# First layer: all picked-expert tiles in one line of pairs behind the last scan; decay and r read from two PSUM banks, rows shifted by one

## What is computed

```python
# attention of layer 0 (RWKV form), per token, 16 heads of 16 x 16:
kv = kt[..., :, None] * vt[..., None, :]
o = einsum('bhk,bhkv->bhv', rt, S + u[None, :, :, None] * kv)
S = dt[..., None] * S + kv
# then group norm, gate, x = x + o @ Wo, h2 = rms_norm(x), x = x + gelu(h2 @ w1) @ w2
# feed-forward of layer 0: 2 shared experts, 4 of 16 routed experts per token
probs = softmax(xt @ router_w.T); topk_p, topk_i = top_k(probs, 4)
routed = einsum('tre,rhe->th', gelu(up_r) * gate[:, :, None], routed_down)
```

## Time and profile before

| | us |
|---|---|
| median of 3 runs | 5062.5 (5051.38 to 5066.56) |
| profiled execution | 5088.27 |
| its span | 5086.5 |
| mean granted PE clock of the span | 0.899 |
| first layer's scans | 52.3 to 2249 |
| second layer's first scan | 2683.7 |
| second layer's scans end | about 4384 |

### The profile page before, as it was taken

One profiled execution on the slowest core, in us unless ns is written; L12 is line 12 of the kernel. 1 busy time (PEld: TensorE's weight loads), 2 busy tenths in 40 slices (PEclk: granted clock), 3 DMA queues, 4 the chain that ended last, 5 costly groups with the idle time before them and its releaser, 6 DMA issues. The chain is left out here.

```text
span 5086.5 us, 64064 instructions
## 1 busy us (share of the span) xinstructions
PE 4041.3 (79%) x19024; PEld 2762.4 (54%) x19024; DVE 3733.9 (73%) x6383; ACT 2719.0 (53%) x5646; POOL 3369.3 (66%) x2370
## 2 busy tenths in 40 slices
PE   5777787887778887878448989888888888489994
PEld 1344554565445654556345555555555555368883
DVE  6888698678886888741008998988889888645677
ACT  1333643454345543546237777777777777245552
POOL 3456576576566766672358888888888888645552
PEclk7888887999889988989679999999999999699997
DMA  4233445444544446641662122221112211396788
GB/s 180 85 102 127 145 134 134 143 146 132 134 146 144 156 129 151 167 154 53 144 152 84 59 68 83 84 72 70 65 67 82 85 67 66 136 237 206 243 279 279
DMA packets 378773, 659.74 MB, mean 130 GB/s; under 512 B 43616, under 2 KB 235488, under 8 KB 368096
## 3 DMA queue, kind: packets, MB, share of 16 engines
q1 hardware_dynamic: 288576, 464.59, 28.7%
q0 software_dynamic: 89856, 191.05, 13.4%
HBM read 455.29 MB, written 250.25 MB: 139 GB/s over the span
## 5 line engine op out<-in xcount | busy, mean ns | idle before, releaser
L1687 POOL TENSOR_TENSOR c_dbx<-c_dtx,c_Brep 128x1024 f32<-128x1024 f32 x512 | 1202.5, 2364 | 183.2 <-DVE c_hs L1705 99.0
L1705 DVE TENSOR_TENSOR_SCAN c_hs<-psum,c_carry,c_dbx 128x512 f32<-128x512 f32 x768 | 937.3, 1266 | 120.0 <-ACT psum L1694 70.7
L1116 POOL TENSOR_TENSOR a_kv<-a_rk,a_kv 128x512 f32<-128x512 f32 x512 | 708.1, 1391 | 431.2 <-DMA a_kv<-v_rows 419.7
L1125 DVE TENSOR_TENSOR_SCAN a_S<-a_decay,a_carry,a_kv 128x513 f32<-128x513 f32 x512 | 804.2, 1571 | 153.3 <-POOL a_kv L1116 147.8
L1694 ACT ACTIVATE psum<-c_dt,c_cols 128x512 f32<-128x512 f32 x1024 | 697.2, 688 | 364.9 <-DVE c_hs L1705 359.2
L1721 PEld LDWEIGHTS psum<-ident,c_hs 128*128 128x128 f32 x4096 | 488.1, 144 | 392.2 <-DVE c_hs L1705 213.8
L1721 PE MATMUL psum<-ident,c_hs 128*128 128x128 f32 x4096 | 611.0, 283 | 108.9 <-DVE c_hs L1705 104.1
L962 POOL DMA_INDIRECT picked_results<-a_t_y,a_to_slot x336 | 386.8, 1151 | 421.4 <-ACT a_t_y L953 165.8
L1131 DVE TENSOR_TENSOR a_prod<-a_rk,a_S 128x512 f32<-128x512 f32 x512 | 454.9, 888 | 78.3 <-PE psum L1147 78.3
L2110 POOL DMA_INDIRECT results<-d_ys,d_to_row x320 | 312.0, 975 | 250.4 <-issue 140.0
L872 POOL DMA_INDIRECT picked_rows<-a_row,a_to_row x256 | 351.8, 1374 | 122.7 <-issue 42.5
(11 more groups left out here) (316 smaller groups left out, 8161.6 us busy)
## 6 DMA issues: line engine op xcount, KB each, us to landing
a_kv<-v_rows SPq DMA_DIRECT2D x512, 256.0 KB
c_Brep<-b_rows SPq DMA_DIRECT2D x64, 1024.0 KB, 4.8
a_t_rows<-picked_rows SPq DMA_DIRECT2D x336, 144.0 KB
d_xs<-sorted_rows SPq DMA_DIRECT2D x320, 128.5 KB
x<-picked_results POOLq DMA_DIRECT2D x64, 512.0 KB, 7.6
d_w<-results SPq DMA_DIRECT2D x64, 512.0 KB, 11.4
d_w<-in_d_experts SPq DMA_DIRECT2D x32, 768.0 KB
picked_rows<-in_picked_pad SPq DMA_DIRECT2D x80, 144.0 KB
```

The costliest lines, as they stand in the source:

```text
L1116: m_kv[g] = pool.mark(nc.gpsimd.tensor_tensor(kv[:, g % NV, 1:C + 1], rk[slot][:, 1, hb, :], kv[:, g % NV, 1:C + 1], ALU.mult))
L1125: m_scan[q] = dve.mark(nc.vector.tensor_tensor_scan(S[:, q % NS, :], decay[cq % 2][:, hb, :], kv[:, q % NV, :], carry[:, sq_:sq_ + 1], ALU ...
L1687: m_dbx[g] = m_dbx[g + 1] = pool.mark(nc.gpsimd.tensor_tensor(dbx[:, r:r + 2, :], dtx[slot][:, e, :].unsqueeze(1).broadcast_to([P, 2, C]), ...
L1705: m_scan[q] = dve.mark(nc.vector.tensor_tensor_scan(hs[:, q % NR, :], psum[:, DA + q % ND, :], dbx[:, q % NX, :], first, ALU.mult, ALU.add))
```

## The change

In the scan loop:

- kv, S and the product are shifted by one token: column 0 of k, v and decay is the last column of the chunk before (three small ACT copies a chunk, one in `rv`, one in `decay`, one in `ks`), a state has 512 columns, and no column 0 is kept apart.
- For each block of 16 steps ACT copies decay and r (128x512) into PSUM banks 6 and 5. The first 3 steps of a block (`COPIED`) read SBUF as before, the other 13 the banks.
- Keeping the carry goes from DVE to ACT.
- kv, S and prod have 8 buffers each, the fetch runs 5 steps ahead, `PACE` is 3200.
- The pool `G` has 3 banks (1, 2, 7) instead of 5.

Tiles:

- `SEGMENTS` = 8, 8: 144 tiles a segment, 288 in all, in 144 pairs. `tiles` is gone from the background. `pairs_of_tiles` runs behind the last scan, a straight line with one pair per iteration, stages shifted against each other, one bank for each of its four products. The copies of the rows and of the hidden transposes go from ACT to DVE. Twice an iteration it advances the background once: the last chunk's block, the combines of chunks 0 to 7, and the second layer's opening, which begins when chunk 0 is combined.
- The combines of chunks 8 to 15 go into the second layer's scan loop. That layer waits for every tile's result to be stored (`wait_left`), and for the sums of a chunk only when it loads that chunk.

The diff, cut:

```diff
-        NV, NS, NP = 6, 4, 6
-        kv, S, prod = brief("kv", [P, NV, C + 1]), brief("S", [P, NS, C + 1]), brief("prod", [P, NP, C])
+        NV, NS, NP = 8, 8, 8
+        kv, S, prod = brief("kv", [P, NV, C]), brief("S", [P, NS, C]), brief("prod", [P, NP, C])
...
-        OB, FD, G = 0, Banks(psum, 2, 1), Banks(psum, 3, 5)
+        FD, G, OB, RB, DB = Banks(psum, 0), Banks(psum, 1, 2, 7), 3, 5, 6
...
+            if c >= 1:
+                act.after(*scanned, *m_done["ready", c - 1])
+                act.mark(nc.scalar.copy(decay[slot][:, :, 0], decay[1 - slot][:, :, C]))
+                m_edge = act.mark(nc.scalar.activation(ks[slot][:, :, 0], ks[1 - slot][:, :, C], ACT.Copy, scale=chunk_mask[:, c:c + 1]))
...
+            m_v = act.mark(nc.scalar.copy(rv[1 - slot][:, :, 0], vT[:, :, C]))
...
+            def rows_turned(p):
+                i, bank = TB.take(pe)
+                pe.engine.wait_ge(s_tx[p % NTX], 32 * (p // NTX + 1))
+                for k in range(2):
+                    for kb in range(KB):
...
+                dve.after(m_y.get(p - NTX))
+                m_of[p] = dve.mark(nc.vector.tensor_copy(t_of[:, p % NTX, :, :], t_rows[:, p % NTX, :, D:]))
+                dve.after(m_T[p], m_up.get(p - 2))
+                m_xT[p] = TB.freed[i] = dve.mark(nc.vector.tensor_copy(t_xT[:, p % 2, :, :].rearrange("p k d -> p (k d)"), bank))
...
+            AHEAD = NTX - 1
+            for p in range(AHEAD):
+                fetch(p)
+            for s in range(total + 2):
+                if s < total:
+                    rows_turned(s)
                 if s >= 2:
...
+                    hidden_turned(s - 2)
+                pause()
+                if 1 <= s <= total:
+                    up(s - 1)
+                if s >= 2:
+                    down(s - 2)
+                    if s - 1 in begins:
+                        m_done["tiles", segment[s - 2]] = s - 1
+                if s + AHEAD < total:
+                    fetch(s + AHEAD)
+                pause()
...
-        CHAIN_RATE, BEFORE_RATE, NORM_RATE, SORT_RATE, LEAD = 3, 1.3, 1.5, 1.0, 3
-        PACE = 4400
+        CHAIN_RATE, BEFORE_RATE, NORM_RATE, SORT_RATE, LEAD = 3, 1.3, 1.5, 1.0, 5
+        PACE, COPIED = 3200, 3
...
-                    m_kv[g] = pool.mark(nc.gpsimd.tensor_tensor(kv[:, g % NV, 1:C + 1], rk[slot][:, 1, hb, :], kv[:, g % NV, 1:C + 1], ALU.mult))
+                    m_kv[g] = pool.mark(nc.gpsimd.tensor_tensor(kv[:, g % NV, :], ks[slot][:, hb, 0:C], kv[:, g % NV, :], ALU.mult))
...
+                    if v < COPIED:
+                        decays = decay[cq % 2][:, hb, 0:C]
+                    else:
+                        decays = psum[:, DB, :]
+                        dve.after(m_bank["decay"])
...
+                    m_scan[q] = dve.mark(nc.vector.tensor_tensor_scan(S[:, q % NS, :], decays, kv[:, q % NV, :], carry[:, sq_:sq_ + 1], ALU.mult, ALU.add))
...
-                    m_prod[q] = dve.mark(nc.vector.tensor_tensor(prod[:, q % NP, :], rk[cq % 2][:, 0, sq_ // DK, :], S[:, q % NS, 0:C], ALU.mult))
+                    m_prod[q] = dve.mark(nc.vector.tensor_tensor(prod[:, q % NP, :], r_t, S[:, q % NS, :], ALU.mult))
...
-                    dve.after(m_scan[q])
-                    m_kept[q] = dve.mark(nc.vector.tensor_copy(carry[:, q % steps - 3:q % steps + 1], S[:, q % NS - 3:q % NS + 1, C]))
+                    act.after(m_scan[q], m_start[0])
+                    m_kept[q] = act.mark(nc.scalar.copy(carry[:, q % steps - 3:q % steps + 1], S[:, q % NS - 3:q % NS + 1, C - 1]))
+                for name, lag, bank, source, m_read in (("decay", 3, DB, decay, m_scan), ("r", 4, RB, rs, m_prod)):
...
+                        m_bank[name] = act.mark(nc.scalar.copy(psum[:, bank, :], source[cq % 2][:, hb, 0:C]))
...
+        tail_done = [("plan", len(Z.SEGMENTS) - 1), ("scattered", last), ("out", last), ("final", 0)]
...
+            left.advance_all()
+            if is_done(*tail_done) and not is_done("second"):
...
-            wait_stored(sp.engine, 2)
             load_xa(0)
...
-            background = Background((AFTER_RATE, []), (MAIN_RATE, []), (SORT_RATE, []), (1.0, []), (1.0, []))
+            background = Background((AFTER_RATE, []), (MAIN_RATE, []), (SORT_RATE, []), (1.0, []), (1.0, []), (1.0, sums))
...
-            wait_stored(lane.engine)
+            wait_left(lane.engine)
...
-    SEGMENTS = [2, 3, 4, 4, 3]
+    SEGMENTS = [8, 8]
```

359 lines of the change are left out of this document (150 added, 209 removed).

## The result

The changed kernel takes **5007.8 us** (median of 4 runs, 5005.5 to 5009.0) against 5063.2 of the kernel before in the same comparison, a ratio of 0.989 [0.988, 0.991]. It is faster, but by 55 us (1.1%) where the forecast said 240, and lies above the forecast's range.

What follows compares the result with a forecast made beforehand. DVE was taken to bound the scan loop's quiet windows, PE some other stretches, no engine the whole. Scan loop -405, stretch between the scans +155, second layer +10 make -240 us: 4824 us, range 4671 to 4970.

Steps and rivals of the forecast that it cites:

- Tiles leave the loop, -0.25 us a step: Scan loop: without tiles and combines the step falls from 4.29 to 4.04 us, read from four tile-free windows.
- Banks, -0.20 and -0.21 us a step: Scan loop: 13 of 16 scans and products reading PSUM save 0.20 and 0.21 us a step.
- Carry to ACT, -0.09: Scan loop: moving the carry's copy off DVE saves 0.09 us a step; ACT has room for it.
- Wider rings: Scan loop: eight buffers give back some of the 0.15 us a step that products waited for PE's sums.
- The pool of three, between 0 and all: Scan loop: three background banks instead of five cost between nothing and all that the other edits save.
- 2.95 us of work: Scan loop: DVE's work falls to 2.95 us a step; with 0.55 of idle kept, the step is 3.5 us.
- the first rival: Scan loop: DVE alone sets the step at 3.2 us, giving 4671 us; chance 0.18.
- The budget: Scan loop: with 3200 columns a step, PE needs 3.6 us in packed stretches, so 3.5 is just possible.
- First half of the pairs, 266 us: Between the scans: 72 pairs at 3.0 us plus 50 us for the last chunk's block; range 228 to 290.
- Second half, 290 us: Between the scans: 72 pairs, 32 sums and the second layer's opening, bound by DMA; range 263 to 381.
- Second layer, +10 us: Second layer's scan loop: 32 sums moved in cost 10 us, bounds 0 and 41.
- idle banks: Scan loop: rival that held-up scans and products stay at 1.52 and 0.93 us, giving 5028 us; chance 0.05.

Runs made afterwards that it cites:

- e9: Kernel before with only the tiles and combines out of the scan loop, rows shifted by one token, and the changed kernel's work behind the last scan: 5195 us.
- e3: Changed kernel without the copies to the banks, so all scans and products read SBUF; pool of 3 kept: 5104 us.
- e6: Changed kernel with rings back at 6, 4 and 6 buffers and fetches 3 steps ahead: 5011 us.
- e2: Changed kernel with the old budget, PACE 4400 columns a step instead of 3200: 5180 us.
- e1: Changed kernel with the carry's copy back on DVE: 4974 us.
- e15: e11 with two more rests lengthened (five in all), banks serving 14 of 16 steps, and the carry's copy on ACT: 4867 us.
- e7: e1 with three background rests lengthened (centring matmul, gate's product, head norm's last product): 4968 us.
- e11: e7 with rings of 6, 4 and 6 buffers and fetches 3 steps ahead: 4946 us.
- e16: Changed kernel with five background rests lengthened and nothing else: 4897 us.
- e5: e3 with the two freed banks given to the background's pool, five instead of three: 5087 us.
- e18: Kernel before the change with the same five rests lengthened: 5073 us, ratio 1.002.

## Why the prediction was wrong, point by point

- *Tiles leave the loop, -0.25 us a step.* Too much: -0.15 (e9), 53 us of the loop. Half of the error is in how the windows were averaged: the first, 400 of 1050 us, lies at the start of the loop, where steps are short, and by its share of the loop they give 4.09 and not 4.04. The other half stays open.
- *Banks, -0.20 and -0.21 us a step.* The prices of the instructions were right (1274 and 665 ns), and so was their sum, 0.42. The rule of the Trainium skill weighed there (Perfetto Trace Analysis, Optimizing Scalar/DVE Operations), about 60 ns for a DVE access on SBUF and 125 on PSUM, so 65 ns more as an estimate, does not show: a product takes 665 ns in the mean from a bank, and 654 and 662 are the shortest and the median from SBUF (e3). It does not hide between instructions either: from the start of a product that is not held to that of the next scan are 581 ns with banks and 583 without (medians, after and e3). DVE's work still ended at 3.09 instead of 2.95. That is not the banks' failure, which took off 0.45: the base was higher, 3.54 in e3 where the forecast's terms give 3.45 - 0.09 = 3.36. Of this the wide rings hold about 0.05 (e6), and 3200 columns instead of 4400 go with 0.10 (e2).
- *Carry to ACT, -0.09.* Wrong in sign: undoing it gains 34 us in this kernel (e1). The forecast named the work queued behind the waiting copy, and put its cost at nothing, since ACT "has the room". It is nothing only when the rests are long (e15).
- *Wider rings.* Named as a gain without a number; they give none (e6), and cost 21 us with three rests lengthened (e7, e11) and about 30 with all five (e15, e16).
- *The pool of three, between 0 and all.* About 15 us, near the lower bound (e5).
- *2.95 us of work and "I keep 0.55" of idle time.* This is the step that failed. Work came out at 3.09 and idle time at 0.68, each about half of the 0.26 us by which the step was missed. DVE's idle time does not stay when work is taken from beside it. Most of it is waiting for results of ACT and PE that are asked for a fixed number of steps after their inputs, and a shorter step asks sooner: from e3 to after, with the same rests, the four waits for gate, a_o, a_rv and a_ha rise from 142 to 229 us. So 0.45 us less of work brought 0.18 in the step and 0.27 of idle. Edit by edit the step went from 4.29 to 4.14 (tiles, e9), 3.94 (budget, rings, carry and pool, e3) and 3.76 (banks); the forecast had 4.04, 3.91 and 3.50, so that the banks' term is the one that fell short most, by 0.23, against 0.10 for the tiles and 0.07 the other way for the rest. The forecast said of the first rival that this idle time "is mostly waiting for ACT and PE, which gain nothing", and then did not let it grow. With the rests lengthened the step is 3.54 (e16), 0.04 from the forecast's 3.5, with DVE at 3.08 + 0.45.
- *The budget.* The forecast used it only to ask if PE fits. It was worth 178 us of loop (e2), the largest single effect. The step of 4.04 stood for the loop at 4400 columns, and no term said what 3200 would gain.
- *First half of the pairs, 266 us.* Right: the first pair's last ACT stage began at 2006.8, and 72 pairs were stored by 2275, 268 us. Two small errors cancel in it: pairs alone take 2.8 us instead of 3.0, and the last chunk's block so has some 66 us instead of 50.
- *Second half, 290 us.* 323: 5.5 us a pair beside the sums for 150 us, with a DMA share of 1.10, so DMA bound it as forecast, but then 3.9 us a pair for 175 us at a DMA share of 0.45, while PE was busy 84%, in part with the second layer's opening. That work was named and given no time in the sum. Around the pairs it was 45 us instead of 34.
- *Second layer, +10 us.* +14.

Of the 185 us between forecast and result (240 - 55), 135 are the loop (405 - 270) and 43 the stretch (198 - 155), by the profiled executions; the rest is in the loop of the second layer and in how the profiled execution of before stood to its median. Of the rivals none came true as written: the banks did what they are for, PE did not take DVE's place, and pairs and sums did overlap in part. The time landed near that of idle banks, 5028, for another reason.

## What to carry to other kernels

When work is taken from an engine that runs in order, ask for each remaining wait how many steps lie between an operation and its input: rests that are counted in steps of a loop shrink with the step, and have to be lengthened together, since a few alone mostly move the wait to the next place. That paid here only once DVE had room for it: the same five gave nothing in the kernel before (e18). When a loop is priced from windows in which some work is absent, compare the windows with each other first, and weigh each by its share of the loop. And before held time on the operations left is put down to an edit, look at the same operations, place by place, in the kernel without the edit.
